# First linear-attention stage of a four-layer kernel: denominators left in PSUM, and three reorderings on VectorE, ScalarE and GpSimd

## The reference

```
q, k, v = split(x @ w.T)                       # 16 heads of 8
k_exp  = exp(k * scale) + 1e-06
k_norm = cumsum(k_exp, over the tokens)
qs     = softmax(q * scale, over the head's 8) / k_norm
carry  = carry + k_t[:, None] * v_t[None, :]   # token by token, an 8x8 state per head
y_t    = einsum(qs_t, carry)
out    = y @ w_out
```

## Time and profile before

| what | us |
| --- | --- |
| median of three runs | 731.29 |
| the profiled execution, its whole time | 734.08 |
| the profiled execution's span | 732.3 |
| PE, DVE, ACT, POOL busy in the span | 607.4, 535.0, 398.1, 385.4 |
| of the stretch 60 to 165 us (105 us): PE, DVE, POOL, ACT busy | 94.56, 93.34, 90.18, 60.57 |

### The profile page before, as it was taken

One profiled execution on the slowest core, in us unless ns is written; L12 is line 12 of the kernel. 1 busy time (PEld: TensorE's weight loads), 2 busy tenths in 40 slices (PEclk: granted clock), 3 DMA queues, 4 the chain that ended last, 5 costly groups with the idle time before them and its releaser, 6 DMA issues.

```text
span 732.3 us, 14471 instructions
## 1 busy us (share of the span) xinstructions
PE 607.4 (83%) x4113; PEld 365.8 (50%) x4148; DVE 535.0 (73%) x1869; ACT 398.1 (54%) x834; POOL 385.4 (53%) x537
## 2 busy tenths in 40 slices
PE   2598999986006999999987888999999999998994
PEld 2354555554003687777765344445454545453543
DVE  4478898996881454554789798698989898987454
ACT  2456565541802222235422567677777777767772
POOL 0377888884017788768855643334343434333341
PEclk9889999999557999999999799899999999999997
DMA  9920000000401223434642340221112121100111
GB/s 304 272 42 0 2 1 0 0 0 1 128 19 52 50 46 58 84 52 77 100 66 26 77 66 4 41 29 41 29 35 37 31 38 29 43 3 4 31 53 34
DMA packets 44522, 36.72 MB, mean 50 GB/s; under 512 B 4192, under 2 KB 39568, under 8 KB 44448
## 3 DMA queue, kind: packets, MB, share of 16 engines
q1 hardware_dynamic: 34112, 27.83, 16.4%
q0 software_dynamic: 8992, 7.38, 7.1%
q10 hardware_dynamic: 1344, 0.62, 0.3%
HBM read 13.93 MB, written 8.91 MB: 31 GB/s over the span
## 4 chain that ended last, share of the span: by engine, by line
PE 48%; DVE 18%; issue 7%; ACT 3%; POOL 1%; DMA 0%; DVEq 0%; ACTq 0%; POOLq 0%
DVE rows_home L1785 9%; PE bank L2171 9%; PE wide L1313 7%; PE bank L1321 7%; PE wide L2158 6%; PE bank L2093 4%; PE wide L1331 3%; PE wide L2093 2%; PE bank L2183 1%; DVE st L301 1%; PE bank L2068 1%; DVE slot_t L876 1%; ACT L276 1%; DVE slot_v L874 1%; PE bank L1305 1%
## 5 line engine op out<-in xcount | busy, mean ns | idle before, releaser
L1948 ACT ACTIVATE pexp<-wide 128x512 f32<-128x512 f32 (+2 forms) x384 | 181.5, 537 | 79.5 <-PE wide L2158 76.4
L1878 POOL TENSOR_SCALAR_AFFINE_SELECT pexp<-pexp 128x256 f32<-128x256 f32 x256 | 106.1, 418 | 174.2 <-ACT pexp L1948 172.2
L1785 DVE CUSTOM_DVE_ANT_0 rows_home<-bank,mask_qk 128x384 f32<-128x384 f32 (+3 forms) x326 | 142.0, 482 | 13.1 <-PE bank L2093 12.0
L2158 PE MATMUL wide<-qT,kTe 128*128 128x256 bf16 (+3 forms) x501 | 120.7, 303 | 7.1 <-DMA qT<-rows_home 2.4
L1296 ACT ACTIVATE hT<-wide,b1T 128x512 f32<-128x512 f32 x64 | 43.8, 686 | 129.0 <-PE wide L1313 129.0
L1785 DVE CUSTOM_DVE_ANT_0 rows_home<-wide,mask_qk 128x512 f32<-128x512 f32 (+3 forms) x186 | 86.8, 493 | 25.2 <-PE wide L2093 25.1
L1044 POOL DMA_INDIRECT x_dram<-yg,row_u x48 | 75.9, 1582 | 33.7 <-DVE yg L1094 21.2
L1036 POOL DMA_INDIRECT x_row<-xln_dram,row_u x64 | 63.2, 988 | 52.6 <-DVE slot_tok L905 33.4
L2093 PE MATMUL bank<-kTm,qT 128*128 128x384 bf16 (+3 forms) x318 | 77.1, 306 | 14.3 <-DVE rows_home L1785 11.0
L2171 PE MATMUL bank<-pexp,vx 128*32 128x512 f32 (+3 forms) x1024 | 85.4, 446 | 0.5 <-POOL pexp L1878 0.5
L2158 PEld LDWEIGHTS wide<-qT,kTe 128*128 128x128 bf16 x512 | 48.8, 99 | 42.6 <-ACT pexp L1948 20.7
(11 more groups left out here) (278 smaller groups left out, 993.5 us busy)
## 6 DMA issues: line engine op xcount, KB each, us to landing
qT<-rows_home SPq DMA_DIRECT2D x144, 64.0 KB
qT<-kTm SPq DMA_DIRECT2D x3, 1024.0 KB, 15.2
x_sb<-in_L_attn_x SPq DMA_DIRECT2D x8, 256.0 KB, 6.6
w_sb<-in_L_ffn_w SPq DMA_DIRECT2D x1, 2048.0 KB, 12.5
xln_dram<-rows_home SPq DMA_DIRECT2D x8, 256.0 KB, 2.2
out_x<-x_sb SPq DMA_DIRECT2D x7, 256.0 KB, 2.3
x_dram<-x_sb SPq DMA_DIRECT2D x6, 256.0 KB, 2.8
x_sb<-x_dram SPq DMA_DIRECT2D x6, 256.0 KB, 3.2
```

What stands on the lines that cost most here:

```text
L1785: ins = nc.vector.tensor_tensor_reduce(out=masked[:, n % 4, at], in0=bank_of(n)[:, at], in1=mask_qk[:, T - w:T], scale=1.0, scalar=LEAST, ...
L1878: nc.gpsimd.affine_select(out=pexp[:, at, :, 0:P], in_=pexp[:, at, :, 0:P], pattern=[[0, 2], [1, P]], compare_op=ALU.is_ge, fill=0.0, base ...
L1948: nc.scalar.activation(pexp[:, exp_slot(b, 2 * step + h // 2), h % 2:h % 2 + nh, 0:w], scores_bank(b, m)[:, 0:nh * w].rearrange("p (h t) - ...
L2158: ins = nc.tensor.matmul(scores_bank(b, m)[:, hh * w:(hh + 1) * w], kTe[:, par, j * P:(j + 1) * P], qT[:, b % QB, 4 * qd + h + hh, j * P:T ...
```

## The change

The buffer `den` in SBUF goes away. The denominator is written back into `psK` (bank 0), where the key sums are; the Newton step's first half works in place there, ACT's logarithm and the second half read it from there. PE's next key sums wait for qs (L410) instead of for the denominator.

On DVE, the first reduction of a turn goes ahead of `qmax`; the statistics of the layer norm are taken a turn later, between that reduction and `qmax`; qs (L410) goes ahead of the fourth reduction. On ACT, `qe` and the load of the logarithm's table go ahead of the normalised x of two sequences on (`xln`, L495), and the explicit preset of the exponential's table is dropped (the load remains, in front of the exponential). On POOL, the third outer product goes behind the next sequence's keys, key sums and shift.

```diff
-        den = scratch("den", [P, NT, D])
+        den = psK[:, :].rearrange("p (k d) -> p k d", d=D)
...
         def dve_lin_den(dve, b):
...
-            dve.wait_ge(a_qs.sem, a_qs.at(b, 0))
-            nc.vector.tensor_tensor(by_head(den[:, :, :]), psK[:, :].rearrange("p (kh l) -> p kh l", l=L),
+            nc.vector.tensor_tensor(psK[:, :].rearrange("p (kh l) -> p kh l", l=L), psK[:, :].rearrange("p (kh l) -> p kh l", l=L),
                                     qsum[:, :].unsqueeze(2).broadcast_to([P, NT * HEADS, L]),
                                     ALU.mult).then_inc(a_den.sem, 1)
...
-        def dve_lin_turn(dve, b, par, tail=True, front=True):
+        def dve_lin_turn(dve, b, par, tail=True, front=True, before=True):
             dve_lin_prod(dve, b, 0)
+            dve_lin_reduce(dve, b, 0)
+            if before:
+                dve_lin_stats(dve, b - 2)
             if front:
                 dve_lin_qmax(dve, b + 1, 1 - par)
-            dve_lin_reduce(dve, b, 0)
...
-                dve_lin_stats(dve, b - 1)
             if front:
                 dve_lin_qsum(dve, b + 1)
                 dve_lin_den(dve, b + 1)
+            else:
+                dve_lin_stats(dve, b - 1)
...
             if front:
                 dve_lin_residue(dve, b + 1)
+                dve_lin_qs(dve, b + 1)
             dve_lin_reduce(dve, b, 3)
-            if front:
-                dve_lin_qs(dve, b + 1)
...
         def act_lin_seed(act, b):
-            act_preset(act, ACT.Ln)
...
-            act_preset(act, ACT.Exp)
...
+            if front:
+                act_lin_qe(act, b + 1)
+                act_preset(act, ACT.Ln)
             if front and ahead:
                 act_lin_xln(act, b + 2)
             if front:
-                act_lin_qe(act, b + 1)
                 act_lin_seed(act, b + 1)
...
-            pool_lin_outer(pool, b, par, 2)
             if front:
                 pool_lin_keys(pool, b + 1, 1 - par)
                 pool_lin_key_sums(pool, b + 1, 1 - par)
                 pool_lin_shift(pool, b + 1, 1 - par)
+            pool_lin_outer(pool, b, par, 2)
             pool_lin_outer(pool, b, par, 3)
...
         def pe_lin_key_sums(pe, b, par):
-            pe.wait_ge(a_den.sem, a_den.at(b, 0))
+            pe.wait_ge(a_qs.sem, a_qs.at(b, 0))
```

More of the change, by code:

```diff
@@ L400, in dve_lin_residue @@
             dve.wait_ge(a_den.sem, a_den.at(b, 1))
-            nc.vector.scalar_tensor_tensor(out=den[:, :, :], in0=den[:, :, :], scalar=-1.0, in1=seed[:, :, :],
+            nc.vector.scalar_tensor_tensor(out=den, in0=den, scalar=-1.0, in1=seed[:, :, :],
                                            op0=ALU.mult, op1=ALU.mult).then_inc(a_left.sem, 1)
@@ L409, in dve_lin_qs @@
             dve.wait_ge(a_qsTp.sem, a_qsTp.at(b, 0))
-            nc.vector.scalar_tensor_tensor(out=qs[:, :, :], in0=den[:, :, :], scalar=2.0, in1=qe[:, :, :],
+            nc.vector.scalar_tensor_tensor(out=qs[:, :, :], in0=den, scalar=2.0, in1=qe[:, :, :],
                                            op0=ALU.add, op1=ALU.mult).then_inc(a_qs.sem, 1)
@@ L476, in lin_dve @@
             dve_lin_qs(dve, 0)
-            dve_lin_turn(dve, 0, 0, tail=False)
+            dve_lin_turn(dve, 0, 0, tail=False, before=False)
             dve_inverse(dve, B // 2, B, "ln1_second")
             dve_shift_of_mean(dve, B // 2, B)
-            dve_lin_turn(dve, 1, 1)
+            dve_lin_turn(dve, 1, 1, before=False)
             for i in range(1, B // 2 - 1):
@@ L520, in act_lin_seed @@
         def act_lin_seed(act, b):
-            act_preset(act, ACT.Ln)
             act.wait_ge(a_den.sem, a_den.at(b, 1))
             act.wait_ge(a_qs.sem, a_qs.at(b, 0))
-            nc.scalar.activation(seed[:, :, :], den[:, :, :], ACT.Ln).then_inc(a_log.sem, 1)
-            act_preset(act, ACT.Exp)
+            nc.scalar.activation(seed[:, :, :], den, ACT.Ln).then_inc(a_log.sem, 1)
             act.wait_ge(a_log.sem, a_log.at(b, 1))
```

## The result

The changed kernel takes 737.59 us, the median of 11 runs (735.79 to 738.27); the kernel before, run between them, 734.12, also of 11. One of these 11 took 837.04 us, a slow run, and only the other ten (727.93 to 734.86, mean 732.2) enter the ratio. The ratio is 1.0071 with a 95% interval of 1.0046 to 1.0096: about 5.2 us slower (3.4 to 7.0), and less than 1 per cent. The medians alone lie 3.5 us apart. The profiled execution took 737.64 us.

What follows compares the result with a forecast made beforehand. The prediction took a ring of DVE's gapless half and PE's half, 17.46 us a turn, as the bound. Terms 3.1 + 1.3 - 0.5 - 0.4 + 1.2 = +4.7 us on 731.29 gave 736.0 us, range 729 to 743.

Steps and rivals of the forecast that it cites:

- DVE's half: DVE's gapless work from first reduction to end of fourth products: 10.72 us, becoming 11.34 with qmax's 0.62 inside it.
- turn 0: In turn 0 ACT's four normalisations come in front of the logarithm, with almost no other gap: +1.3 us.
- turn 6: Turn 6 has no normalisations, and POOL's masked state, which the next reduction awaited, comes 0.4 earlier: -0.4 us.
- The ring goes through ACT now: ACT's late logarithm (8.05) delays PE's outer sums to 11.72, later than DVE's 11.54: turn 18.26 against 17.48, +0.78.
- the ring: Dependency loop from one turn's first reduction to the next, through DVE, then PE: 10.72 + 0.20 + 6.54 = 17.46 us.
- PE's slack: PE's spare 1.3 us before the third products need their outer sums: used up, transposes of x at about 10.9, not 10.30.
- The denominator in PSUM at nothing: DVE writing the denominator into PSUM costs 0; DVE's 0.95 us saved a turn falls in idle time, booked 0.
- writes to PSUM: Slower rival: +0.61 on each of seven denominators in DVE's gapless half, +4.3 more, 740.3 us; chance 0.15.
- The faster rival: The first reduction no longer waits for PE, DVE's own work becoming the turn: 722 to 725 us; chance 0.1.
- PE's half: PE's part of the turn, from first outer sums through yT matmuls to the next first reduction: 6.54 us, untouched by the change.
- No change: Rival: unseen slack takes up qmax's 0.62 and turn 7's statistics lie in a wait: 730 to 733 us; chance 0.2.
- move as a block: The stages behind the first attention begin when it ends and shift with it, so its +4.7 us reaches the total.

Runs made afterwards that it cites:

- qmax_alone: The kernel before with only the maximum of the queries moved behind the first reduction: 737.39 us, ratio 1.0065.
- qmax_back: The changed kernel with the maximum of the queries back in front of the first reduction: 730.55 us, ratio 0.9968.
- xln_back: The changed kernel with ACT's four normalisations back in front of qe: 737.15 us, ratio 1.0056.
- filler: The changed kernel with six extra matmuls, whose result nobody reads, in PE's idle time ahead of the third outer sums: 737.12 us, ratio 1.0064.
- den_only: The kernel before with the denominator and the Newton step in PSUM and nothing else: 730.61 us, ratio 0.997.
- best_den_sbuf: stats_early_last with the denominator back in an SBUF buffer: 726.34 us, ratio 0.9909.
- halves: stats_early_last with the first half of a turn's first outer sums waiting only for the first half of the last products: 723.13 us, ratio 0.986.
- stats_early_last: The changed kernel with statistics and maximum ahead of the first reduction, POOL's and ACT's order back, last statistics behind the last reduction: 719.57 us, ratio 0.9821.

## Why the prediction came out as it did

The forecast was +4.7 us, the measurement +5.2 (3.4 to 7.0). The mechanism of DVE's half held; the step through ACT did not, and two terms were off in opposite directions. In the stage itself the two profiled executions differ by 148.47 - 142.32 = 6.15 us, 1.45 more than forecast, and the closeness of the totals is in part luck. By terms:

| term | forecast | measured |
| --- | --- | --- |
| turn 0 | +1.3 | +1.41 |
| turn 1 | -0.5 | -0.63 |
| turns 2 to 5 | +3.1 | +3.58 |
| turn 6 | -0.4 | +0.61 |
| turn 7 | +1.2 | +1.18 |

**DVE's half.** Right to 0.01 us where the clock did not fall: from the first reduction to the end of the fourth products it is 91.86 + 1.28 - 81.81 = 11.33, forecast 11.34. `qmax_alone` and `qmax_back` show that this is the cause.

**"The ring goes through ACT now".** This step failed. The logarithm started at 7.84, not 8.05, and `tT` ended at 10.73, not 10.98: the four normalisations hold ACT for 1.54, and the logarithm read from PSUM takes 0.57 for 0.63. PE's transposes were at 10.88, not 11.1, and the outer sums followed 0.50 behind them, at 11.38, not 11.72; that is 0.05 behind DVE's last product. The 0.20 that the prediction had there belongs to turn 3 alone (its); turns 1, 2 and 4 of the kernel before have 0.05 or 0.06. Its 17.46 joins the first half of turn 3 to the second half of turn 2, and so meets the mean partly by chance: turn 2 is 10.90 + 0.05 + 6.54 = 17.49, turn 3 is 10.72 + 0.20 + 6.76 = 17.68. DVE's half sets the ring: in `xln_back` the transposes of turn 3 start 10.70 behind the first reduction, and the outer sums still 0.05 behind DVE's last product, with no shorter undisturbed turn. The three undisturbed turns are 18.05 in the mean, +0.57 for the +0.78 forecast. The price given for this case, "+0.6 even if ACT and PE were in time", was the true one; four turns of it are 2.3 and not 3.1.

**The clock.** Missing from the prediction. It put the third outer sums at 6.2 us (measured 87.98 - 81.81 = 6.17, 4.91 before) and counted them against PE's slack only; it did not ask what PE does meanwhile, which is nothing, for 2 us. The longest hole in the regular turns before was 0.94 us (1.68 in turn 1 and 1.86 in turn 7), with no fall; of the five of the changed kernel, 1.99 to 2.08 us long, two were followed by one. Turn 4 lost about 1.4 us and turn 6 about 1.2, the latter turning its -0.4 into +0.61: without it the turn is 16.25 in `filler`, forecast 16.4. Together the falls cost 2.6 us in this execution, three times the 0.8 by which the ring was overestimated.

**Turn 0.** The size was nearly right (1.15 of the 1.41 lie behind `qe`, the other 0.26 ahead of it where the prediction has nothing), the cause half of it: ACT's order and POOL's hold that turn up side by side, as the runs with one and with both undone show.

**The denominator in PSUM at nothing.** Right. It costs 0.700 us for 0.692, the two operations behind it 0.69 each, the outer products 1.95 throughout; the rival "writes to PSUM" falls, and turn 6's gain in `den_only` is what remains. The Trainium skill (SBUF — State Buffer, "Who interferes with whom") says that a DVE instruction with two SBUF inputs and a GpSimd instruction that reads SBUF wait for one another. The traces agree: in `best_den_sbuf` qs, 2.27 us long, ends at 109.77, 0.56 behind the end of GpSimd's outer product beside it (106.81 + 2.40). What the wait is worth depends on the order: 0 us a turn in one, 0.7 in the other.

**The faster rival** fell in the changed kernel, as its condition was named: PE's half stayed at 6.55 us (99.74 - 93.19). It came true in `best_den_sbuf`, by the other door: DVE was made ready later. **No change** falls as well: each undisturbed turn from 2 to 5 is longer than the same turn before, by 0.44 to 0.60 us.

**The whole.** The spans differ by 3.6 us, not by the 6.3 that the stage ends later. Behind the stage the kernel before has 550.3 us in its profiled execution and the changed one 547.6; the other kernels have 545.5 to 547.8, but for `filler` (548.8) and `halves` (550.3), though nothing there was changed. So "move as a block" holds to 3 to 5 us only. What goes with the difference is the clock. By stretch, the kernel before first, then the changed kernel:

```profile
460.00:470.00 10.00, 9.97 (x70) 5.03 (x69) 5.35 (x23) 5.65 (x12) 2.37 (x7) 0.74 0.13 32
```

```profile
460.00:470.00 10.00, 6.94 (x60) 3.71 (x54) 4.67 (x19) 7.76 (x17) 2.17 (x6) 1.00 0.00 2
```

The kernel before has a fall here, 276 to 284 us behind the end of the stage, that the changed kernel does not have; `halves`, the other kernel with 550.3, has it at the same distance, and none of the others has it. Timed runs say the same: in the runs of the kernel before that were made beside the experiments (727.87 to 735.84 us), every run up to 732.78 has a mean granted clock of 0.948 or more, every one above it 0.946 or less. Which of the two an execution gets is not explained. It is why a step of 2 us, as in `den_only`, is read here from the stage and not from the total.

## What to carry to other kernels

Find the ring that closes from turn to turn and mark on each engine which part of its work lies in it without a gap; an instruction moved from that engine's waiting part into the gapless part costs its full length, however much work the same change saves elsewhere. Work of the gapless part that has no deadline (here the statistics) belongs into the wait: with it there, and the denominator in PSUM, the turn went from 17.48 to 16.09 us (16.87 with the denominator in SBUF). When a producer gets later, look also at the hole that it leaves on TensorE, not only at the slack, for the matmuls behind it may run at half the clock.

## What the runs showed of the hardware

- TensorE's clock can fall to its lower level behind an idle time of about 2 us in the midst of dense work, for about 3 us, with four matmuls of 1.98 us taking 3.40 in the changed kernel; but three of its five such holes had no fall. The length of the hole alone does not decide: in `qmax_alone` the clock fell behind one of 1.57 us and not behind one of 2.35. The runs don't tell what does.
- Six extra matmuls per turn in the hole kept the clock at 1.00 and cost the ring nothing in turns 2 to 5 (17.94 to 18.23), but a later hole then had the fall.
- VectorE multiplying 128x512 in place in one PSUM bank takes 700 ns, against 692 from PSUM into SBUF. ScalarE's logarithm of 128x512 takes 574 ns from PSUM (median, changed kernel) and 630 from SBUF.
- A VectorE operation with two SBUF inputs, beside GpSimd's outer products, and just behind another such operation, took 2.27 us for 0.69, the outer product beside it 2.40 for 1.95 (`best_den_sbuf` against `stats_early_last`).
